# Attention heads stacked by component instead of interleaved, with the softmax shifts moved by four small DMAs

## The reference

```python
x = x + L0_attn(layernorm(x)); x = x + L0_xattn(ctx, layernorm(x)); x = x + L0_ffn(layernorm(x))
x = x + L1_attn(layernorm(x)); x = x + L1_xattn(layernorm(x), ctx, ctx); x = x + L1_ffn(layernorm(x))
```

```python
def L1_attn(x):                                    # 512 queries, 512 keys
    q, k, v = (heads(x @ W.T + b) for W, b in ...)  # [head, token, 16]
    w = softmax(einsum('bshd,bzhd->bhsz', q, k) / sqrt(16))
    return einsum('bhsz,bzhd->bshd', w, v) @ Wo.T + bo

def L1_xattn(query, key, value):                   # 512 queries, 1024 keys
    q, k = rope(heads(query @ Wq.T + bq)), rope(heads(key @ Wk.T + bk))
    attn = softmax(einsum('bhqd,bhkd->bhqk', q, k) * 16 ** -0.5)
    return (attn @ v) @ Wo.T + bo
```

## Time and profile before

| | us |
|---|---|
| three executions | 2193.52, 2196.21, 2197.28 |
| median | 2196.21 |
| the profiled execution's own time | 2193.52 |
| its span, first to last instruction | 2191.7 |
| PE busy in it | 1975.8 (90%) |
| DVE busy | 1726.2 (79%) |
| ACT busy | 1348.8 (62%) |
| POOL busy | 263.0 (12%) |

### The profile page before, as it was taken

One profiled execution on the slowest core, in us unless ns is written; L12 is line 12 of the kernel. 1 busy time (PEld: TensorE's weight loads), 2 busy tenths in 40 slices (PEclk: granted clock), 3 DMA queues, 4 the chain that ended last, 5 costly groups with the idle time before them and its releaser, 6 DMA issues.

```text
span 2191.7 us, 42867 instructions
## 1 busy us (share of the span) xinstructions
PE 1975.8 (90%) x17926; PEld 1123.7 (51%) x17926; DVE 1726.2 (79%) x2680; ACT 1348.8 (62%) x2001; POOL 263.0 (12%) x279
## 2 busy tenths in 40 slices
PE   1899988989989997989999998898998999889898
PEld 1577652423656774232466766333265777533235
DVE  7888878695888887789588887868767888786856
ACT  3566656487356665848536664666944666565782
POOL 2000001341000001035100000103400000011410
PEclk9999999999999999999999999999999999999999
DMA  6165620020036670001005665001001656400100
GB/s 267 37 131 125 132 61 1 1 81 27 20 78 123 126 138 20 2 28 71 11 20 116 129 125 114 1 2 78 21 11 41 124 120 130 90 1 1 78 2 10
DMA packets 416416, 147.64 MB, mean 67 GB/s; under 512 B 403544, under 2 KB 411872, under 8 KB 415328
## 3 DMA queue, kind: packets, MB, share of 16 engines
q1 hardware_dynamic: 415648, 142.82, 27.9%
q0 software_dynamic: 576, 2.10, 0.3%
HBM read 41.86 MB, written 2.10 MB: 20 GB/s over the span
## 4 chain that ended last, share of the span: by engine, by line
PE 64%; DVE 25%; ACT 6%; issue 3%; DMA 2%; POOL 0%; POOLq 0%; SPq 0%; DVEq 0%; ACTq 0%
PE ps L618 12%; DVE nmx L1935 11%; PE ps L620 11%; PE ps L619 11%; PE ps L965 6%; PE ps L780 4%; PE ps L951 3%; PE ps L774 3%; PE ps L775 3%; PE ps L1032 3%; DMA arena<-arena 2%; PE ps L920 2%; DVE arena L1747 1%; DVE st L1579 1%; PE ps L975 1%
## 5 line engine op out<-in xcount | busy, mean ns | idle before, releaser
L1935 DVE TENSOR_REDUCE nmx<-ps 128x2 f32<-128x1024 f32 x384 | 446.8, 1219 | 31.4 <-PE ps L920 29.3
L1444 ACT ACTIVATE arena<-ps 128x512 f32<-128x512 f32 x768 | 406.3, 600 | 49.7 <-PE ps L951 45.3
L618 PE MATMUL ps<-arena 128*128 128x512 f16 (+1 forms) x800 | 272.9, 341 | 1.3 <-DVE arena L1671 0.8
L619 PE MATMUL ps<-arena 128*128 128x512 f16 (+1 forms) x800 | 272.8, 341 | 0.0
L620 PE MATMUL ps<-arena 128*128 128x512 f16 (+1 forms) x800 | 272.6, 341 | 0.0
L1734 DVE TENSOR_SCALAR_CACHE_REDUCE ps<-ps 128x1536 f32<-128x1536 f32 x128 | 225.8, 1764 | 43.0 <-PE ps L620 42.5
L965 PE MATMUL ps<-arena 128*17 128x256 f32 x3072 | 240.1, 389 | 0.0
L1747 DVE SCALAR_TENSOR_TENSOR arena<-arena,rs 128x1536 f16<-128x1536 f32 x128 | 231.6, 1810 | 4.2 <-ACT arena L1338 4.2
L1338 ACT ACTIVATE arena<-arena,rs 128x1536 f16<-128x1536 f32 x128 | 200.8, 1568 | 40.1 <-DVE rs L1740 40.1
L1331 ACT ACTIVATE arena<-ps,nm 128x1536 f32<-128x1536 f32 x128 | 197.1, 1540 | 8.5 <-DVE ps L1734 8.5
L590 POOL TENSOR_TENSOR rstd<-ve,col 128x2 f32<-128x2 f32 x40 | 29.3, 733 | 1307.3 <-DVE ve L1840 874.8
(11 more groups left out here) (285 smaller groups left out, 3798.6 us busy)
## 6 DMA issues: line engine op xcount, KB each, us to landing
arena<-in_experts SPq DMA_DIRECT2D x4, 3840.0 KB, 11.5
arena<-in_weights SPq DMA_DIRECT2D x8, 929.0 KB, 12.3
arena<-in_ctx SPq DMA_DIRECT2D x4, 1024.0 KB, 5.2
arena<-arena SPq DMA_TRANSPOSE x256, 3.2
arena<-in_ctx_t SPq DMA_DIRECT2D x4, 1024.0 KB, 4.7
arena<-in_ternary SPq DMA_DIRECT2D x2, 1024.0 KB, 5.7
y<-in_x POOLq DMA_DIRECT2D x4, 512.0 KB, 4.3
x<-in_x SPq DMA_DIRECT2D x4, 512.0 KB, 3.7
```

Of the source, the lines that this page charges most:

```text
L618: mm(out_, lh, rh, start=(k == 0), stop=False)
L619: mm(out_, lh, rl_, start=False, stop=False)
L1444: A(pr_[:, n % RING, :], ps[:, 4 + n % 3, :], ACT.Exp).then_inc(b_exp.sem, 1)
L1935: V.tensor_reduce(nmx[:, g_ % 2, ch, :, pp, i], ps[:, 2 * (z % 2):2 * (z % 2) + 2, :], AX.X, ALU.max, negate=True)\
```

## The change

The stacked layout changes. Before, a head's 64 partitions were 16 columns times 4 interleaved parts, of which the fourth held the shift. Now they are three runs of 16 partitions, then two partitions (48 and 49) for the high and low half of the shift, and 14 that hold zeros. The selection matrices are written accordingly, in runs of 16 elements. `nm32` and `sh_lo` are gone. The shift slot transposes 16 columns of `nmx` itself. In mode 0 no copy precedes it and it no longer waits on `nm_done`; in mode 1 the smaller of the two halves is written in place. `shift_split` works on 16 partitions. SP now issues four DMAs for each shift, each from 8 partitions of `sh` into one partition of `qs`.

```diff
-HC = 3
+HR = 48
+SR = HR + 2
...
-                    sp.dma_start(qs[HC:P:32, 2 * g_:2 * g_ + 2, :], sh[0:32, g_ % 2, :]).then_inc(sh_in.sem, 16)
+                    for e in range(2):
+                        for part in range(2):
+                            r0 = 64 * e + HR + part
+                            sp.dma_start(qs[r0:r0 + 1, 2 * g_:2 * g_ + 2, :], sh[8 * e:8 * e + 8, g_ % 2, part, :])\
+                              .then_inc(sh_in.sem, 16)
...
-                pe.wait_ge(nm_done.sem, nm_done.at(b, GROUPS * mode.m + g_ + 1))
+                if mode.nch == 2:
+                    pe.wait_ge(nm_done.sem, nm_done.at(b, g_ + 1))
...
-                mm(ps[0:32, 2 * (z % 2), 0:P], nm32[:, g_ % 2].rearrange("p e r n -> p (e r n)"), ident[:],
+                mm(ps[0:16, 2 * (z % 2), 0:P], nmx[:, g_ % 2, 0].rearrange("p e c i -> p (e c i)"), ident[:],
...
-                    pe.wait_ge(sh_in.sem, sh_in.at(b, 16 * (GROUPS * mode.m + g_ + 1)))
+                    pe.wait_ge(sh_in.sem, sh_in.at(b, 64 * (GROUPS * mode.m + g_ + 1)))
...
-                if (a + 1) % mode.per_group == 0:
+                if mode.nch == 2 and (a + 1) % mode.per_group == 0:
                     dve.wait_ge(sl_free.sem, sl_free.at(b, mode.slot0 + z + 1))
-                    by_ch = [...]
-                    if mode.nch == 2:
-                        last = TT(nm32[:, g_ % 2], by_ch[0], by_ch[1], ALU.min)
-                    else:
-                        last = TS_(nm32[:, g_ % 2], by_ch[0], 1.0, None, ALU.mult)
-                    last.then_inc(nm_done.sem, 1)
+                    both_ch = nmx[:, g_ % 2].rearrange("p k e c i -> p k (e c i)")
+                    TT(both_ch[:, 0], both_ch[:, 0], both_ch[:, 1], ALU.min).then_inc(nm_done.sem, 1)
...
-                src, dst = ps[0:32, 2 * (z % 2), 0:P], sh[0:32, g_ % 2, :]
-                own.link(TS_(dst, src, 1.0 / 64.0, None, ALU.mult))
-                STT(dst, src, sh_lo[0:32], dst, ALU.mult, ALU.subtract).then_inc(sl_free.sem, 1)
+                src = ps[0:16, 2 * (z % 2), 0:P]
+                own.link(TS_(sh[0:16, g_ % 2, 0, :], src, 1.0 / 64.0, None, ALU.mult))
+                STT(sh[0:16, g_ % 2, 1, :], src, 1.0 / 64.0, sh[0:16, g_ % 2, 0, :], ALU.mult, ALU.subtract)\
+                    .then_inc(sl_free.sem, 1)
...
-                dst = sel[:, kind].rearrange("p j (e d r) -> p j e d r", e=2, d=LD)[:, :, :, :, r_]
+                dst = sel[:, kind].rearrange("p j (e n) -> p j e n", e=2)[:, :, :, LD * r_:LD * r_ + LD]
```

More of the change, by code:

```diff
@@ L151, in decoder @@
         nmx = sb("nmx", [P, 2, 2, 2, 2, NT])
-        nm32 = sb("nm32", [P, 2, 2, 2, 2 * NT])
         sums = sb("sums", [P, 4])
@@ L158, in decoder @@
         k_pad = sb("k_pad", [P, 1])
-        sh_lo = sb("sh_lo", [P, 1])
-        ARENA = 96 * 1024 + 512
+        ARENA = 97 * 1024
         arena = sb("arena", [P, ARENA // 4])
@@ L254, in decoder @@
         assert lay.at == 98304
-        sh = lay.take([2, P], F16)
+        sh = lay.take([2, 2, P], F16)
         lay = Layout()
@@ L321, in decoder @@
         ones_set = sig("ones_set", 1)
-        sl_mm, sl_free, nm_done = sig("sl_mm", 2 * 112), sig("sl_free", 110), sig("nm_done", 2 * GROUPS)
-        sh_in = sig("sh_in", 2 * GROUPS * 16)
+        sl_mm, sl_free, nm_done = sig("sl_mm", 2 * 112), sig("sl_free", 110), sig("nm_done", GROUPS)
+        sh_in = sig("sh_in", 2 * GROUPS * 64)
         b_mm, b_exp, pv_mm = sig("b_mm", 192), sig("b_exp", 192), sig("pv_mm", 8 * 48)
@@ L1936, in max_slot @@
                     .then_inc(sl_free.sem, 1)
-                if (a + 1) % mode.per_group == 0:
+                if mode.nch == 2 and (a + 1) % mode.per_group == 0:
                     dve.wait_ge(sl_free.sem, sl_free.at(b, mode.slot0 + z + 1))
-                    by_ch = [nmx[:, g_ % 2, k].rearrange("p e c i -> p e (c i)").unsqueeze(2).to_broadcast([P, 2, 2, 2 * NT])
-                             for k in range(mode.nch)]
-                    if mode.nch == 2:
-                        last = TT(nm32[:, g_ % 2], by_ch[0], by_ch[1], ALU.min)
-                    else:
-                        last = TS_(nm32[:, g_ % 2], by_ch[0], 1.0, None, ALU.mult)
-                    last.then_inc(nm_done.sem, 1)
+                    both_ch = nmx[:, g_ % 2].rearrange("p k e c i -> p k (e c i)")
+                    TT(both_ch[:, 0], both_ch[:, 0], both_ch[:, 1], ALU.min).then_inc(nm_done.sem, 1)
             def shift_split(b, mode, g_):
@@ L1950, in shift_split @@
                 if n >= 2:
-                    dve.wait_ge(sh_in.sem, sh_in.at(b, 16 * (n - 1)))
+                    dve.wait_ge(sh_in.sem, sh_in.at(b, 64 * (n - 1)))
                 dve.wait_ge(sl_mm.sem, sl_mm.at(b, 2 * (mode.mm0 + z + 1)))
-                src, dst = ps[0:32, 2 * (z % 2), 0:P], sh[0:32, g_ % 2, :]
-                own.link(TS_(dst, src, 1.0 / 64.0, None, ALU.mult))
-                STT(dst, src, sh_lo[0:32], dst, ALU.mult, ALU.subtract).then_inc(sl_free.sem, 1)
+                src = ps[0:16, 2 * (z % 2), 0:P]
+                own.link(TS_(sh[0:16, g_ % 2, 0, :], src, 1.0 / 64.0, None, ALU.mult))
+                STT(sh[0:16, g_ % 2, 1, :], src, 1.0 / 64.0, sh[0:16, g_ % 2, 0, :], ALU.mult, ALU.subtract)\
+                    .then_inc(sl_free.sem, 1)
             def slots(b, mode, a0, a1):
@@ L2136, in _ @@
             own.mark(TS_(taps[:], col[:, COL["cw"]:COL["cw"] + 3 * NM], mw[:, 0:1], None, ALU.mult))
[L2137 to L2144, removed]
+            pad = ident[:].rearrange("p (e n) -> p e n", e=2)[:, :, HR:SR]
+            own.link(V.tensor_reduce(k_pad[:], pad, AX.XY, ALU.add))
+            own.link(TS_(k_pad[:], k_pad[:], 64.0, None, ALU.mult))
             dve.wait_ge(b2_hi.sem, 1)
```

## The result

The changed kernel takes 2224.35 us (median of 4 executions, 2221.53 to 2230.80) against 2195.28 us (4 executions, 2193.52 to 2197.28). The ratio is 1.0146, with a 95% interval of 1.0126 to 1.0167. It is slower by 29 us. The forecast was 2196.5 us, between 2190.8 and 2202.0. It was wrong by 28 us. Of its chances, 0.14 lay on slower, and no rival named the main cause. The record holds ten further executions of the changed kernel, from 2222.68 to 2236.08 us; the median of all fourteen is 2227.2, 32 us above the kernel before.

A forecast was written before the change was run, and what follows sets the result against it. The prediction took PE (64% of the chain) alternating with DVE (25%) as the bound. Its terms, -0.7 - 1.6 - 0.2 + 2.8 = +0.3 us, on the median 2196.2 gave 2196.5 us, range 2190.8 to 2202.0.

The forecast's parts named there:

- the start: Program start on DVE: fewer small instructions for sh_lo and cheaper sel copies save 0.7 us, between 0.45 and 1.0.
- mode 0: First attention mode: dropping the copy into nm32 saves 0.4 us a batch row, 1.6 us in four (1.2 to 2.4).
- mode 1: Second attention mode: the minimum over 16 columns instead of 32 saves 0.2 us, between 0 and 0.5.
- the four DMAs: Each shift's split on SP: the last part lands 3.15 us after the first issue, costing 2.8 us (1.2 to 4.0).
- p: Time between two successive shift DMA issues on SP, taken as 0.50 us, between 0.38 and 0.56.
- 0.65 that I had named as a sign of being wrong: Shift DMA issues on SP: standing over 0.65 us apart would show the prediction wrong.
- landing of 1.65 us: One shift DMA, from the start of its issue on SP to its signalled landing: 1.65 us.
- last shift of mode 1: Last shift of each batch row, room 2.50 us: PE stands still 0.7 us, four times, +2.8 us.
- First shift of mode 1: covered: First shift of mode 1, room 3.07 us: 0.13 us late, hidden by PE's 0.52 us wait for DVE, cost 0.
- The other six: 0: The other six shifts of a batch row, with room of 3.60 us or more: no wait, cost 0.
- Rival 1: Shift DMAs: issues slower than 0.56 us make shifts late at more places; at 0.70, +11.2 us, 2204.9 us; chance 0.11.
- Rival 3, the clock: Whole kernel: half-clock stretches decide, each up to 1.7 us; two fewer give 2193.1 us, two more 2199.9; chance 0.15.

The follow-up runs named there:

- experiment 1: The changed kernel with 32 unused bytes ahead of arena, so that it starts on a multiple of 256 bytes: 2201.35 us, ratio 1.0031 to the kernel before.
- experiment 2: The kernel before with 224 unused bytes ahead of arena, nothing else changed: 2219.11 us, ratio 1.0112.
- experiment 3: The kernel before with each shift sent in four DMAs, of 8 rows each into one partition: 2205.86 us against 2194.12, ratio 1.005.
- experiment 4: The changed kernel with arena on a multiple of 256 bytes and two DMAs a shift instead of four: 2195.02 us, ratio 1.0006 to the kernel before.
- experiment 9: The same kernel as experiment 4, timed again with more executions: 2193.93 us against 2194.79 for the kernel before, ratio 0.9996.
- experiment 5: The kernel before with 32 unused bytes ahead of arena: 2218.77 us against 2193.79, ratio 1.011.
- experiment 6: The kernel before with 128 unused bytes ahead of arena: 2217.17 us, ratio 1.0103.

## Why the prediction was wrong

- **The step that failed first: the sum held only the steps that the change touches.** Its parts are the start, mode 0, mode 1 and the four DMAs, and everything else is put at zero without a reason. The removal of two small tensors was priced by the instructions that went with them, not by what lies behind them in memory. It moved `arena` off a multiple of 256 bytes, and 256 transposes in a block with no edit at all became 0.5 us slower. Cost: 22 to 25 us of the 29, shown from both sides (experiments 1 and 2). With the address put right, the changed kernel takes 2201.35 us, inside the range. The lines of the change have both facts in them, the tensors taken away and the `arena` behind them.
- **The four DMAs: right mechanism, wrong size.** I had p = 0.50 us, up to 0.56, and measured is 0.68, beyond the 0.65 that I had named as a sign of being wrong. With it the last part lands 3.72 us after the first issue instead of 3.15. The landing of 1.65 us itself was right (1.68 in the chain). At the last shift of mode 1 PE loses 1.27 us instead of 0.7. The arguments for p were shapes with many rows, taken as an upper bound; the one shape that mattered, a single partition, was in no row, and it was the slowest. The 674 ns of the first shift lay nearest, but by chance: it is one slow issue out of 32 of the old shape.
- **"First shift of mode 1: covered": right, and with more to cover than forecast.** From issue to first use it is 3.86 us instead of 3.07, so the first turned scores come 0.8 us later where I had 0.13. But PE's next score slots had been waiting for DVE, 0.5 us each, and no longer do. Before, behind the one of the earlier trace rows, and then after:

```profile
453.15 0.39 PE L920 MATMUL ps<-arena 64*128 64x512 f16 x2 [0.52 <-DVE nmx L1935]
454.28 0.39 PE L920 MATMUL ps<-arena 64*128 64x512 f16 x2 [0.53 <-DVE nmx L1935]
```
```profile
459.23 0.39 PE L924 MATMUL ps<-arena 64*128 64x512 f16 x2
460.32 0.39 PE L924 MATMUL ps<-arena 64*128 64x512 f16 x2
461.46 0.39 PE L924 MATMUL ps<-arena 64*128 64x512 f16 x2
```

  Counted from the issue of the shift, the slots come at 3.97, 5.10 and 6.23 us before and at 4.07, 5.16 and 6.30 after. In experiment 3 the exponentials behind this start are 0.8 us late at the first and no longer at the ninth. The cost is 0 to within 0.1 us.
- **"The other six: 0": nearly.** Four of them had 3.60 to 3.63 us of room, and there the first turned scores come 0.15 to 0.17 us later. Most of it is made up again; what stays in experiment 3 is about 0.2 us a batch row. With the last shift the stalls are 1.5 us a row, 6 us in four, against 2.8 forecast. Rival 1 named the right p but reckoned 11.2 us, since it gave up the cover at the first shift and counted the small losses in full. That its 11.2 is near the 11.7 measured for the split is luck: the stalls in the trace are 6, and at least a part of the rest goes with a lower clock.
- **The start: right.** 0.8 us against 0.7. The copies of `sel` fell from 0.15 to 0.10 us each, 0.32 us together, near the middle that I took and not at the lower end of 0.06 each.
- **Mode 0 and mode 1: right in their stages, not told in the whole.** Mode 0 became 2.2 us shorter in four batch rows, where I had 1.6 (1.2 to 2.4). The slot's waits fell from 6.9 to 4.3 us there. In mode 1 I had 0.2, and nothing can be seen. In the whole, experiments 4 and 9 bound the gain at between 4 us and nothing, and experiments 1 and 3 differ by 4.5 us in its favour. Whether 2.5 us is there stays open.
- **Rival 3, the clock: part of the remainder.** The kernel before with its address moved loses 23 to 25 us at a mean granted clock of 0.984 to 0.989 (experiments 2, 5 and 6), close to its own 0.984 to 0.990, so the clock is not needed to explain those. But the kernels with four DMAs a shift ran at a lower one on the whole: 0.983 to 0.986 in experiment 3, 0.982 to 0.987 in experiment 1, and 0.977 to 0.986 in the fourteen executions of the changed kernel. In the two profiled executions it was 0.986 before and 0.980 after. An estimate from these means: (1 - 0.980) x 2232.0 less (1 - 0.986) x 2191.7 is 14 us, the most that the clock can have added to the 40 us by which the profiled execution was longer. Why it was lower stays open.

The parts add up: about 25 us for the address and 11.7 for the split with its lower clock, less the gains of 0 to 4.5, is 32 to 37 us, beside 29 by the median of four executions and 32 by that of all fourteen. Experiment 1, the changed kernel without the address, is 7.2 us above its before, and with 25 makes 32.

## What to carry to other kernels

A change's diff in memory is as real as its diff in instructions. Whenever a tensor is added, removed or resized, work out the new start of everything allocated behind it, and look whether a DMA reads there; where the chain runs through such DMAs, half a microsecond each is enough. And a DMA split in n parts lands n - 1 issues later, and the price of an issue has to be measured on the part's own shape: here the parts of one partition took longer to issue than the whole of four.

## What the runs showed of the hardware

- A DMA transpose within SBUF whose source tile starts off a multiple of 256 bytes lands 3.7 us after its issue instead of 3.2, at offsets of 32, 128 and 224 bytes alike, and its issue on SP takes about 1434 ns instead of 1405. The offset of the destination by 32 bytes changed neither.
- This agrees with the Trainium skill ("DMA: Bandwidth & Descriptors", section "How a descriptor splits into AXI transactions"), which says that a read has to begin at an address aligned to 256 bytes, so that one which does not also fetches the bytes from the boundary below. By that rule a 256-byte run across a boundary needs two transactions instead of one. The runs show the price for transposes and that it does not depend on the offset; they do not show the transactions themselves.
- The issue of a copy within SBUF on SP took 526 ns for 32 rows into four partitions, 496 for 16 rows into two and 635 for 8 rows into one. Fewer rows do not make a cheaper issue.
